# Halves of X and of the squared deviations added on GpSimd ahead of LayerNorm's mean and variance products

## What is computed

```python
def _layer(x, wqkv, qs, ksc, wo, lg, lb, w1, b1, w2, b2):
    ...
    x = x + o @ wo
    h = shift_token(x)
    mu = h.mean(-1, keepdims=True)
    var = h.var(-1, keepdims=True)
    h = (h - mu) / jnp.sqrt(var + 1e-05) * lg + lb
    h = h @ w1 + b1
    a, g = jnp.split(h, 2, axis=-1)
    h = a * jax.nn.gelu(g, approximate=False)
    x = x + h @ w2 + b2
    return x
```

## Time and profile before

| | before |
|---|---|
| median of 3 runs | 3978.5 us (3974.77 to 3979.97) |
| the profiled execution | 3978.39 us |
| its span, first to last instruction | 3976.5 us |
| PE busy | 3792.9 us, 95% |
| PE weight loads busy | 2553.4 us, 64% |
| DVE busy | 2785.0 us, 70% |
| ACT busy | 2342.7 us, 59% |
| POOL busy | 785.9 us, 20% |
| granted clock, mean | 0.978 |

### The profile page before, as it was taken

One profiled execution on the slowest core, in us unless ns is written; L12 is line 12 of the kernel. 1 busy time (PEld: TensorE's weight loads), 2 busy tenths in 40 slices (PEclk: granted clock), 3 DMA queues, 4 the chain that ended last, 5 costly groups with the idle time before them and its releaser, 6 DMA issues.

```text
span 3976.5 us, 63340 instructions
## 1 busy us (share of the span) xinstructions
PE 3792.9 (95%) x22372; PEld 2553.4 (64%) x22372; DVE 2785.0 (70%) x7663; ACT 2342.7 (59%) x5248; POOL 785.9 (20%) x976
## 2 busy tenths in 40 slices
PE   6799999999999999999999999999999999999977
PEld 3556666666666666666666666666666666666655
DVE  3567777777777777777767777777777777777653
ACT  2356566656566655656665656665656665665643
POOL 1121222122222212122112122212122221212100
PEclk6799999999999999999999999999999999999998
DMA  3000000000000000000000000000000000000000
GB/s 120 6 6 6 12 12 12 12 7 7 12 12 12 12 12 6 6 12 12 12 12 7 6 12 12 12 12 7 7 12 12 12 12 12 4 9 7 7 6 8
DMA packets 48402, 48.89 MB, mean 12 GB/s; under 512 B 8716, under 2 KB 46816, under 8 KB 48096
## 3 DMA queue, kind: packets, MB, share of 16 engines
q1 hardware_dynamic: 48096, 44.87, 3.6%
HBM read 35.69 MB, written 8.39 MB: 11 GB/s over the span
## 4 chain that ended last, share of the span: by engine, by line
PE 74%; DVE 15%; ACT 4%; POOL 3%; issue 3%; DMA 0%; SPq 0%; POOLq 0%; DVEq 0%; ACTq 0%
PE ps L976 13%; PE ps L871 9%; PE ps L989 8%; PE ps L885 6%; PE ps L729 4%; PE ps L938 4%; PE ps L918 3%; PE ps L927 3%; PE ps L947 3%; POOL inv L544 3%; PE ps L758 3%; PE ps L786 3%; PE ps L905 2%; PE ps L776 2%; PE ps L811 2%
## 5 line engine op out<-in xcount | busy, mean ns | idle before, releaser
L976 PE MATMUL ps<-feed_area,w_s 128*128 128x256 f32 x2560 | 595.3, 384 | 7.4 <-DVE feed_area L1257 6.3
L544 POOL TENSOR_TENSOR inv<-ssq_f,minus_half 128x16 f32<-128x16 f32 x128 | 419.0, 3273 | 860.7 <-DVE ssq_f L1193 860.7
L642 ACT ACTIVATE attn_area<-attn_area,f_nb,inv 128x128 f32<-128x128 f32 (+1 forms) x1024 | 546.1, 538 | 20.7 <-DVE f_nb L1221 19.9
L976 PEld LDWEIGHTS ps<-feed_area,w_s 128*128 128x128 f32 x2560 | 479.1, 192 | 93.1 <-issue 16.8
L1130 DVE TENSOR_REDUCE c_mx<-ps 128x2 f32<-128x512 f32 x512 | 343.4, 687 | 144.6 <-PE ps L758 141.3
L1217 DVE CUSTOM_DVE_ANT_0 attn_area<-ps,cst 128x128 f32<-128x128 f32 (+1 forms) x1024 | 304.0, 353 | 150.0 <-issue 150.0
L1267 DVE SCALAR_TENSOR_TENSOR feed_area<-ps,b_s,feed_area 128x256 f32<-128x256 f32 (+1 forms) x384 | 184.6, 481 | 272.3 <-ACT feed_area L664 263.1
L595 ACT ACTIVATE cond_area<-ps 128x512 f32<-128x512 f32 x512 | 298.6, 596 | 123.1 <-PE ps L776 118.8
L989 PE MATMUL ps<-feed_area,w_s 128*128 128x256 f32 x1536 | 355.3, 381 | 0.7 <-DVE feed_area L1267 0.7
L633 ACT ACTIVATE attn_area<-ps 128x512 f32<-128x512 f32 x256 | 152.5, 596 | 321.5 <-PE ps L905 318.7
L664 ACT ACTIVATE feed_area<-ps,b_s 128x256 f32<-128x256 f32 x320 | 150.9, 472 | 313.6 <-PE ps L976 313.2
(11 more groups left out here) (150 smaller groups left out, 7062.7 us busy)
## 6 DMA issues: line engine op xcount, KB each, us to landing
x_rows<-in_x SPq DMA_DIRECT2D x32, 256.0 KB, 2.8
f_rows<-in_fside_BxSxS SPq DMA_DIRECT2D x32, 256.0 KB, 3.0
res_rows<-in_x SPq DMA_DIRECT2D x32, 256.0 KB, 2.8
out<-res_rows SPq DMA_DIRECT2D x32, 256.0 KB, 2.2
wqkv_s<-in_L_ffn_wqkv SPq DMA_DIRECT2D x2, 1536.0 KB
w_s<-in_L_ffn_w SPq DMA_DIRECT2D x2, 1364.0 KB
cond_area<-cond_area SPq DMA_DIRECT2D x128, 6.0 KB
w_s<-in_L_ffn_w SPq DMA_DIRECT2D x2, 640.0 KB
```

Source lines behind the costliest of these rows:

```text
L544: nc.gpsimd.tensor_tensor(inv[:, l, t, :], ssq_f[:, l, t, :], minus_half[:, :], ALU.pow).then_inc(SL[l]["inv_norm"], 1)
L642: nc.scalar.activation(soft[:, h % SOFT, lo:hi], soft[:, h % SOFT, lo:hi], ACT.Exp, bias=f_nb[:, l, q, h:h + 1], scale=inv[:, l, q, h:h + ...
L976: last = mm(ps[:, N0 + f % 2, c * N:(c + 1) * N], w1_s[:, l, k, lo:lo + P], hn[:, k, :], start=(k == 0), stop=(k == KD - 1))
```

## The change

GpSimd gets two new steps in each layer. In step "mean" it waits until both halves of X are there, and adds them into `xsum` (128x256). In step "variance" it waits for the squares and adds their halves into `hsum`. PE then needs one product in place of two in each: it waits for `x_added` and `dev_added`, and no longer for `x_attn` and `dev_squared`. `xsum` uses the memory of `rstd_s`, `hsum` that of `std_s`; for `xsum` GpSimd also waits until the previous LayerNorm is done with it (`normed`). The order strings of DVE, ACT and POOL change; that of PE does not.

```diff
-        std_s = feed.take(N)
-        rstd_s = feed.take(N)
+        hsum = std_s = feed.take(N)
+        xsum = rstd_s = feed.take(N)
...
+                elif name == "mean":
+                    both = shifted(X_attn[l])
+                    pool.wait_ge(SL[l]["x_attn"], upto(seq, "x_attn", KD))
+                    was = previous(l, seq)
+                    if was:
+
+                        pool.wait_ge(SL[was[0]]["normed"], upto(was[1], "normed", 1))
+                    nc.gpsimd.tensor_tensor(xsum, both[:, 0, :], both[:, 1, :], ALU.add).then_inc(SL[l]["x_added"], 1)
+                elif name == "variance":
+
+                    pool.wait_ge(SL[l]["dev_squared"], upto(seq, "dev_squared", 1))
+                    nc.gpsimd.tensor_tensor(hsum, hsq[:, 0, :], hsq[:, 1, :], ALU.add).then_inc(SL[l]["dev_added"], 1)
...
                 elif name == "mean":
-                    pe.wait_ge(SL[l]["x_attn"], upto(seq, "x_attn", KD))
...
-                    for k in range(KD):
-                        last = mm(ps[:, N0, 0:N], mean_w[:, :], shifted(X_attn[l])[:, k, :],
-                                  start=(k == 0), stop=(k == KD - 1))
-                    last.then_inc(SL[l]["mean"], 1)
+                    pe.wait_ge(SL[l]["x_added"], upto(seq, "x_added", 1))
+                    mm(ps[:, N0, 0:N], mean_w[:, :], xsum, start=True, stop=True).then_inc(SL[l]["mean"], 1)
                 elif name == "variance":
-                    pe.wait_ge(SL[l]["dev_squared"], upto(seq, "dev_squared", 1))
-                    for k in range(KD):
-                        last = mm(ps[:, N0 + 1, 0:N], mean_w[:, :], hsq[:, k, :], start=(k == 0), stop=(k == KD - 1))
-                    last.then_inc(SL[l]["variance"], 1)
+                    pe.wait_ge(SL[l]["dev_added"], upto(seq, "dev_added", 1))
+                    mm(ps[:, N0 + 1, 0:N], mean_w[:, :], hsum, start=True, stop=True).then_inc(SL[l]["variance"], 1)
```

More of the change, by code:

```diff
@@ L129 @@
     DVE=((65, 16, 22, 0),
-        "RSSRRRNSRRASAASARSSRSSSASSAANASASASSAAAARSRASSAASSNNRNSRANNAARSARNSSSRNNRNRAAARARRANAAASRSSNNNAAANNA"
+        "RSSRRRNSRRASAASARSSRSSSASSAANASASASSAAAARSRASSAASSNNRNRASNNAARSARNSSSRNNRNRAAARARRANAAASRSSNNNAAANNA"
         "NAARSANSSASNASASAAASAAAAASSAASASSAAASSSSAASSAAASAAAAARANAAARA"),
     Activation=((57, 19, 24, 0),
-        "AAAAAARARARRARASNSASASSASRSAAAAANASSSAARSARSRRASNSSNASSRAANRSSSSNNASANRASNNARAAARNAAARAANARSSNNRNSNA"
+        "AAAAAARARARRARASNSASASSASRSAAAAANASSSAARSARSRRASNSSNASSARANSRSSSNNASANARSNNAARAANRAAAARANASRSNNNRSNA"
         "NAAANSAANASRSASASAANASSAASAAAASNASRRRASSSSSAAARASSSRSAASAASAS"),
-    Pool=((54, 11, 29, 1),
-        "NNSNNRRRRRRRRRRRNNNSSNNNSNSSSSSSASASASSASAAAAAAAAASSNNNNAAAAAASSRSSNNNAANSSAAAAARNNSSAASSSSSSSRRRSSS"
-        "SSAAAAAAAAAAARRRRSAAAAAAAAASSSASSASSSRRRRAAAAAAAAAAAAAAAAAASS"),
+    Pool=((65, 16, 22, 0),
+        "NRSSRRRSRRASAASARSSRSSSASSAANASASASSAAAASRSRASSAANSNNNSRANAARRSARNSSSRNNRNRAAARARRANAAASRSSNNNANNANA"
+        "ARSANAASSASNASASAAASAAAAASSASSSASSAAAASSAASSAAASAAARRAAANAAAA"),
 )
@@ L183 @@
     pv=FH, o_copied=HP, wo_out=KD, x_attn=KD,
-    mean=1, centered=1, dev_squared=1, variance=1, std=1,
+    x_added=1, mean=1, centered=1, dev_squared=1, dev_added=1, variance=1, std=1,
     rstd=1, normed=1, w1_out=HK, gelu=HK, geglu=HK,
@@ L538, in layer @@
             def layer(seq, name, n):
-                if name != "rotate":
+                if name == "finish":
                     return
                 l, t = n[0:2]
-                pool.wait_ge(SL[l]["floored"], upto(seq, "floored", t + 1))
-                nc.gpsimd.tensor_tensor(inv[:, l, t, :], ssq_f[:, l, t, :],
-                                        minus_half[:, :], ALU.pow).then_inc(SL[l]["inv_norm"], 1)
+                if name == "rotate":
+                    pool.wait_ge(SL[l]["floored"], upto(seq, "floored", t + 1))
+                    nc.gpsimd.tensor_tensor(inv[:, l, t, :], ssq_f[:, l, t, :],
+                                            minus_half[:, :], ALU.pow).then_inc(SL[l]["inv_norm"], 1)
+                elif name == "mean":
[8 more added lines that the diff above has]
+                    nc.gpsimd.tensor_tensor(hsum, hsq[:, 0, :], hsq[:, 1, :], ALU.add).then_inc(SL[l]["dev_added"], 1)
             def step(seq, name, n):
```

## The result

The changed kernel takes **4014.74 us** (median of 4 runs, 4011.66 to 4020.28); the kernel before, run beside it, 3976.64 us (4 runs, 3972.49 to 3979.97). The ratio is 1.0098, with a 95% interval of 1.008 to 1.0115: slower by 38 us. The prediction said 3972.5 us, with a range that ended at 3986. The profiled execution of the changed kernel took 4011.66 us, span 4009.9 us, so it has 33.3 us more to explain than the 3978.39 us of before.

The account below looks back on a forecast made before the run. PE, busy 95% of the span, was taken as the bound. A round gains 0.12 + 0.43 - 0.34 = 0.21 us, about 6 us over 29 rounds: 3972.5 us, range 3959 to 3986.

Parts of the forecast that it names:

- Layer 1, variance: PE's variance product in layer 1: chain from the mean 3.03 us, sum within it 0.73; layer 1 loses 0.34 us.
- rival 3: Layer 1's second sum: DVE takes the port first, variance 1.1 us later each round, 4004 us; chance 11%.
- The idle time at the variance: PE's idle time ahead of layer 1's variance, put at about 1.2 us in each round.
- Rival 4: PE's clock falls for some us in the new wait of each round, time over 4000 us; chance 3%.
- Layer 1, mean: POOL's sum stands behind layer 0's second power, so PE gets a new wait of 0.3 us at layer 1's mean.
- Layer 0, mean: Sum covered by PE's rows; the turn behind waits for a copy, so 0.12 us saved of 0.44.
- rival 1: Layer 0's copies are no gate: a round gains 0.54 us, 3962 us; chance 14% with its partial forms.
- Layer 0, variance: Sum of squares covered, copy behind it just early enough: 0.43 us saved in a round (0.35 to 0.44).
- The swaps and the ends: Order swaps on the engines counted at nothing; first and last sequences about zero together, 2 us either way.
- The sum: Total over layers: a round gains 0.21 us, some 29 full rounds give 6 us, forecast 3972.5 us.

Follow-up runs that it names:

- short-instruction run: Changed kernel with a 0.06 us single-column write on DVE ahead of the scaling of layer 0's second key tile: 3976.51 us, ratio 1.0.
- the scaling ahead: Changed kernel with DVE's scaling of layer 0's second key tile moved ahead of the subtraction of layer 1's mean: 3972.35 us, ratio 0.999.
- the late variance: Kernel before, no sums on GpSimd, with PE's variance of layer 1 moved behind the value rows of the next sequence: 3958.55 us, ratio 0.9958.

## Why the prediction was wrong, point by point

- **Layer 1, variance: the step that failed.** The sum stood in it at 0.73 us, and measured 1.64 (L558). The prediction had the sum 0.45 us ahead of the scaling by the shown starts and took that for a margin: "Below 0.4 us of slip it costs nothing." The margin never existed. The sum did start first in the trace, by 0.37 us, and still lost; the short-instruction run, with the same 0.38 us, shows that what stands next in the queue matters and not that distance. Nor was there a slip to hope for or to fear: the scaling follows DVE's subtraction by 1.80 us in both traces (2006.65 to 2008.45, 2018.83 to 2020.63), so it moves with the chain. The row that the prediction showed for the port held a warning. L517 has its start at the same 0.01 us as L1185's and is the one that is held up, 1.27 us for its usual 0.20, each of the 29 times that they meet:

```profile
L517 POOL TENSOR_TENSOR m_parts<-m_rest,m_parts x128: 201/203/1275, 51.5 to 3705.9; 128x8 bf16<-128x8 f32 x128
```

  So the slower rival 3 was the case. Its price of 1.1 us in a round was somewhat high: the round is 118.85 - 117.94 = 0.91 us longer than with the scaling out of the way, since the held sum ends 0.59 us after the scaling's end and not 0.73.
- **The idle time at the variance** was put at about 1.2 us, reckoned from starts. Without the conflict it is 0.98 as the profile prints it, and 1.14 by starts (L918 starts at 2003.88 and takes 0.44, L973 starts at 2005.46); with it 1.89 printed and 2.06 by starts, which is the "2 us or more" named as the sign of rival 3. A chain of 3.03 us was forecast and 2.99 measured without the conflict: the links and signals were sized well.
- **The clock.** Rival 4 was set aside with a wait of 1.2 us, and for that length the argument holds (no fall at 0.98 and 1.50 us). But rival 3 makes the wait 1.89 us, and then the clock does fall, 9 times, 15.2 us. The two were priced as if only one could happen; 4004 for rival 3 lacked this part. With what was measured, 3972.35 us without the conflict + 28 x 0.91 + 15.2 is 4013, beside the measured 4014.7.
- **Layer 1, mean.** Forecast: a new wait of 0.3 us. Measured: 0.32 us. The mean starts 0.77 us behind the turn (2017.28 to 2018.05) where it was 0.45 before; the profile prints only 0.17 of it as idle, since the rows overlap on paper. The run with the mean's sum alone shows the same, 0.33 us. The restart adds 0.07 us. Right in kind and in size.
- **Layer 0, mean.** The copies are the gate, as forecast: 0.07 us saved, 0.12 forecast. The turn comes 0.13 us sooner behind the mean, but takes 0.59 us to the next row and not 0.52, a restart that was left out here. The sum beside L1193 (the old L1185) was put at nearly 2 us; it takes 1.64 us in 30 rounds (1.74 in one) and is covered. PE and ACT there:

```profile
2077.54 0.60 PE L970 MATMUL ps<-feed_area,mean_w 128*128 128x256 f32 x2
2078.28 0.66 PE L918 MATMUL ps<-cst,attn_area 128*128 128x128 f32 x4
```

```profile
2077.63 0.59 ACT L646 ACTIVATE attn_area<-ps 128x512 f32<-128x512 f32 x1
2078.11 0.61 ACT L608 ACTIVATE cond_area<-ps 128x512 f32<-128x512 f32 x1
```

  L646 ends at 2078.22, the turn L918 starts at 2078.28: released by the copy. So rival 1 is out.
- **Layer 0, variance.** No wait. The next row comes 0.58 us behind it (0.96 before): 0.38 us saved, 0.43 forecast, and within its bounds. The copy L394 that it waits for ends at 2092.99 + 0.56 = 2093.55, so "just enough" was a little too little. The stretch to layer 1's mean agrees: 0.06 us shorter, though 0.32 us were lost at that mean.

```profile
2093.11 0.60 PE L973 MATMUL ps<-feed_area,mean_w 128*128 128x256 f32 x2
2093.69 0.93 PE L931 MATMUL ps<-attn_area 64*128 64x128 f32 x8
```

- **The swaps and the ends.** Counted at nothing. The swaps are (ratio 1.0002), and behind the last full round 1.4 us are lost, within the 2 us allowed.
- **The sum.** Where the conflict is out of the way the rest of the sum holds: 3972.35 with the scaling ahead and 3976.51 with the short instruction, against 3972.5 forecast and a range of 3959 to 3986. Their round is 117.94 us, 117.85 forecast: a gain of 0.13 us where 0.21 was counted, the missing part being layer 0's two places. The sum's own length was right, 0.72 to 0.73 us, as read from L502. The range failed since it stopped short of rival 3, at 11%. Its price was on paper; its probability rested on the reading of two shown starts.

## What to carry to other kernels

Work moved from PE to GpSimd pays only where PE has other work while the sum is made: here the same 128 sums cost 38 us in the given order, and brought 37 us, against a kernel with the late variance but no sums, once small moves at three places of the orders closed the gap. Before placing a GpSimd operation with SBUF operands, look at which DVE instruction with two SBUF operands stands next in the queue at that time with its waits met, and count its whole duration in; a distance between two shown starts is no cover. And price together those rivals of which one can bring on the other.

## What the runs showed of the hardware

- A GpSimd sum of 128x256 float32 takes 0.72 to 0.73 us alone, 1.64 us when DVE's 128x512 product with two SBUF operands stands next in the queue, and 1.64 us too (1.74 once) when a DVE product of 128x1024 is shown to start 0.16 us ahead of it. When GpSimd has the port, the DVE product grows from 0.68 to 0.89 or 1.02 us. DVE's copies out of PSUM beside it (L1131) don't stretch the sum.
- In the changed kernel the sum ends 0.59 us after the end of the DVE product that held it: about its full 0.72 us of work less 0.1.
- An instruction of 0.06 us ahead of the DVE product turns the outcome round, and so gave 38 us back (4014.74 to 3976.51). That the port is taken before the start that a trace shows is inferred; no trace shows the port itself.
- Behind a wait of 1.89 us on PE, in a round of 119 us that is otherwise busy, the granted clock went to 1.2 GHz for 3.4 us in 9 rounds of 28, and each time cost 1.69 us. With 1.50 us it did so in none of 28. GpSimd's sums are not needed for it: 2.16 us made by repeated squares on ACT do the same.
